# Other orders of steps on four engines in two stages of a fused four-layer transformer kernel

## What is computed

```python
# Layer 1, attention: linear attention with feature map elu(t) + 1
q, k = elu(q) + 1, elu(k) + 1
kv   = einsum('bhnd,bhne->bhde', k, v)
x    = x + (q @ kv / (q . k_sum + 1e-6)) @ w_out.T
# Layer 1, feed-forward: shared gated net on all tokens, one of 8 experts on 256 tokens
sh         = ln(silu(x @ sw1) * (x @ sw2)); shared_out = sh @ sw3 + sb3
x_moe      = x[index_b, index_t]
top1       = argmax(sigmoid(x_moe @ eg_w.T + eg_b) + exp_bias)
weights    = softmax([sigmoid(shared score), expert score of top1])
expert_out = ln(silu(x_moe @ ew1[top1]) * (x_moe @ ew2[top1])) @ ew3[top1] + eb3
final_out  = shared_out.at[index_b, index_t].set(w0 * shared + w1 * expert_out)
# Layer 2, feed-forward (in stage Last): low-rank experts, y = gelu(x A1) B1, A2, B2, weighted by token
# Layer 3, attention part (in Last): x @ W1 + causal depthwise convolution(x, 21 taps) @ W2 + bias
# Layer 3, feed-forward (in Last): 4-bit quantized gated net
xq   = fp4_quant_dequant(x);  h = silu(xq @ wgq.T) * (xq @ wuq.T)
out  = fp4_quant_dequant(h) @ wdq.T
```

## Time and profile before

| what | value |
| --- | --- |
| device time, three runs | 1425.2, 1425.36, 1428.38 us; median 1425.36 us |
| span of the profiled execution | 1426.4 us |
| busy of the span: PE, DVE, ACT, POOL | 1370.7, 1205.4, 1101.6, 283.0 us |
| stage Layer1 in the trace (first step to the last addition to X) | 399 to 550 us |
| stage Attention2 in the trace | 550 to 1178 us |
| stage Last in the trace | 1178 to 1426.4 us |

### The profile page before, as it was taken

The page is one execution under the profiler, slowest core; times in us unless marked ns, Lnnn a source line. Parts: engine busy times, 40 slices in busy tenths (PEclk is TensorE's granted clock), DMA queues, the critical chain, the costliest instruction groups (busy, mean ns, idle before and its releaser), DMA issues.

```text
span 1426.4 us, 25921 instructions
## 1 busy us (share of the span) xinstructions
PE 1370.7 (96%) x9689; PEld 675.9 (47%) x9689; DVE 1205.4 (85%) x2663; ACT 1101.6 (77%) x2071; POOL 283.0 (20%) x239
## 2 busy tenths in 40 slices
PE   5999999999989998999999999999999999999998
PEld 4552332322258885333343333443333345566796
DVE  6898876785389979999999999888888869999997
ACT  4678989899957724888878888888888877887545
POOL 5210010000033321111211011111011113234452
PEclk9999999999999999999999999999999999999999
DMA  4238788767610001000000000000000000000000
GB/s 113 41 92 173 159 193 190 170 134 170 147 57 1 1 1 75 1 1 1 1 1 1 1 1 1 2 1 1 1 2 1 1 30 1 1 9 8 9 16 23
DMA packets 29949, 65.38 MB, mean 46 GB/s; under 512 B 5376, under 2 KB 16896, under 8 KB 28544
## 3 DMA queue, kind: packets, MB, share of 16 engines
q1 hardware_dynamic: 29824, 63.72, 19.0%
HBM read 54.27 MB, written 9.44 MB: 45 GB/s over the span
## 4 chain that ended last, share of the span: by engine, by line
PE 67%; DVE 17%; DMA 5%; POOL 4%; ACT 2%; issue 2%; SPq 1%; DVEq 0%; ACTq 0%; POOLq 0%
PE ps L2028 16%; PE ps L2018 12%; PE ps L516 6%; PE ps L525 6%; PE ps L1997 6%; PE ps L2041 4%; DVE p6ac L2555 3%; PE ps L2008 3%; DMA p1GB<-gscr 2%; PE ps L534 2%; POOL WA L2235 1%; PE ps L2490 1%; POOL WA L2239 1%; DVE st L164 1%; DMA p1R<-tscr 1%
## 5 line engine op out<-in xcount | busy, mean ns | idle before, releaser
L2137 ACT ACTIVATE p4E<-ps,p4mx,p4sc 128x512 f32<-128x512 f32 x512 | 393.4, 778 | 62.6 <-DVE p4mx L2090 60.8
L2085 DVE TENSOR_REDUCE p4mx<-ps 128x2 f32<-128x1024 f32 x205 | 249.7, 1218 | 29.2 <-PE ps L2018 28.1
L2028 PE MATMUL ps<-p4E,p4vn 128*64 128x512 f32 x1024 | 243.0, 599 | 0.2
L2018 PE MATMUL ps<-p4T 64*128 64x512 f16 x1536 | 199.3, 379 | 3.8 <-ACT p4E L2137 3.5
L2160 POOL TENSOR_TENSOR p4vn<-p4v,p4zs 128x512 f32<-128x512 f32 x64 | 66.7, 1042 | 503.4 <-DVE p4zs L2093 469.6
L657 DVE SCALAR_TENSOR_TENSOR p1Pb<-ps,WB,p1GB 128x512 f32<-128x512 f32 x128 | 95.4, 748 | 64.9 <-PE ps L525 55.0
L752 ACT ACTIVATE p1g<-ps,WB 128x1024 f32<-128x1024 f32 x128 | 135.4, 1121 | 12.6 <-PE ps L516 6.6
L516 PE MATMUL ps<-p1R,p1w1s 128*128 128x512 bf16 x512 | 134.0, 381 | 6.4 <-DMA p1R<-tscr 5.3
L2018 PEld LDWEIGHTS ps<-p4T 64*128 64x128 f16 x1536 | 58.3, 94 | 157.1 <-ACT p4E L2137 86.0
L525 PE MATMUL ps<-p1g,WB 128*32 128x512 f32 x512 | 129.1, 601 | 2.9 <-DVE p1Pb L657 2.7
L525 PE MATMUL ps<-xn,WB 128*32 128x512 f32 x256 | 128.3, 602 | 0.2
(11 more groups left out here) (374 smaller groups left out, 2586.0 us busy)
## 6 DMA issues: line engine op xcount, KB each, us to landing
p1GB<-gscr SPq DMA_DIRECT2D x64, 512.0 KB, 7.5
p1R<-tscr SPq DMA_DIRECT2D x64, 128.0 KB, 6.2
gscr<-p1gT SPq DMA_DIRECT2D x16, 256.0 KB, 6.8
tscr<-p1tp SPq DMA_DIRECT2D x24, 128.0 KB
WB<-in_w SPq DMA_DIRECT2D x1, 2560.0 KB, 9.1
X<-in_x SPq DMA_DIRECT2D x8, 256.0 KB, 5.7
out<-X SPq DMA_DIRECT2D x7, 256.0 KB, 2.3
WA<-in_w SPq DMA_DIRECT2D x4, 438.5 KB, 8.6
```

Source lines behind the costliest of these rows:

```text
L2018: y = p.e.matmul(ps[:, banks[hh], :], t[rows, q, 128 * j:128 * j + 128], t[rows, 2 + r, :], start=o == 0, stop=o == 2)
L2028: t = p.e.matmul(ps[64 * hh:64 * hh + 64, self.bank["ctx", n], :], vn[n % 2][:, j, 64 * hh:64 * hh + 64], E[2 * (n % 2) + hh][:, j, :], st ...
L2085: v.e.tensor_reduce(m, ps[:, low:low + 2, :], AX, ALU.max).then_inc(v.own.h, v.one())
L2137: a.e.activation(self.E[2 * i + hh][:, j, :], ps[:, banks[hh], :], ACT.Exp, bias=self.mx[i][:, j, hh:hh + 1], scale=pre.sc[:, 1, 0:1], acc ...
```

## The change

Eight strings change, four in Layer1 (PE, DVE, ACT, POOL) and four in Last. Each new string has the same letters as the old one as often as before, so that each engine issues the same steps; SP's strings, the steps themselves, the waits that each carries and the numbers of filler products are untouched. The items of a step keep their order. What changes besides the order is what hangs on it: the PSUM bank of each PE step, and where ACT's tables change (in Layer1 and at the start of Attention2 the table loads go from 7 to 5, since the router's sigmoid and exponential now stand otherwise among silu and the rest, and the load ahead of L2137 is no longer needed; in Last they go from 12 to 8).

```diff
--- before.py
+++ after.py
@@ -1019,17 +1019,17 @@
     }
     ORDER = {
         "tensor": (
-            "abcccccccddeabfaegbccccccfeghfhccgdddhbaabiejcccccciciiiifiieagfhbiigejhfiijddgbahiibiiaeiiijifjeiigfhiigjkhkk"
-            "iiiiiiiijljlkmnnlommmmmmmnolknkklknlnlklnnlpppnppqqqqrrrqqqrrrq"),
+            "cbcaccccedcccfbcdcaabgccecehfdfdcbagagbedechfahdfbegiicafhigiehdjijrgbiabiifcchiipkigiceijifjikrhgcchiijikkill"
+            "iiiiikiniijijiiiinlmmooklmlnjmkmknmmnmlkllnnlnppnppqqqrqqrqqrqr"),
         "vector": (
-            "sstcsutvwcccctxexcccsuyztwuescccccytzweshytzhAccBhcAAwiuBiBiiieiisccccccucciwtyzeicccicicyzuhiiwecihcyziAciiBi"
-            "wiihAiuiBiwiAeciuByzecyzhiiiiiiiAhACBCDBDEECFDmCEnmmmmmmmmmmmnDonEmmmmoooCnDoCEDCoEnCoDnDoEEoConnDpEnppppxqrxx"
-            "rqxrrxxrqqrqqqq"),
+            "cscscscutcwectscytzcswuvutewciceccchcyztycsziwiiiuiuAteewyshBzuhAiywezBtyuAhizehcBiixiiiwiAcciiAyzciuciBhBiwie"
+            "AiCBDyzEChcDihcAciiiEAcBiCiCicDciiiBDiEcxFECcmmnDmmcoEnooocommComDCmnDEonCDmmEnEomCmcDoomEcpnmnmnnmcppppcqxrqx"
+            "rxqrxrxqxrqqqqr"),
         "scalar": (
-            "aGtbHtIdtdaGbHIaGtgbHItgtgdddBbHaGIaBBGIbHjtccccccccccccccccccccccccccccgIaGcbHgjccjddgbHBIaGbHBIcaGcjBjggjkkB"
-            "Bkjlljkmlommmmmmmmmmmolkkklkllkllppprrrrrr"),
+            "cbcHaGItdctdbHacccGIIabcGcgHcttdtrbdHaGIaIGgbHdcgtaIGccBdbHcgaIGBgtjjcdcbHccgpcaIbGccHBBkcgkcjjgBckBjkclBcBjkc"
+            "jrlmmcmoccmmolkljkcmmlklkmmlmlmcmlcppcrrrr"),
         "gpsimd": (
-            "csssccccccccsssccccccccAJAAJJsccccccccAJAJAJAADJDJDDDDoooooooDDDrrrr"),
+            "csccscccsccosocossAccccJAscAcAcAcAJccccDoDoJcAJDcAcJcDJJDDJDooDDrrrr"),
         "sync": (),
     }
 
@@ -2258,18 +2258,18 @@
     }
     ORDER = {
         "tensor": (
-            "aabcddbecedeefegeceebdgheeeibdcfejgjjjeedeidcejgfeeedkkblkkjmejgcjeeedefgcckkeeeikdkjjjmjebgfeeedekgkkkibmjjjj"
-            "ldifjjkkjjkkbdmdifjjjjkkkkdmdifjjjjkkkkmijjjjkkkkmkkXkkX"),
+            "abacdbceedbfeeedceeecggeeededhibfjjjjeegceeegeedciljjkjjkfeeekddkbmeedfcggeebikkdjjjjceeefdeeeggdiblkjjfkjmkij"
+            "kdjjkjkjmkdikfbkjjjkjdmdifkkkjjjjkmkkikjkjmkjjkkkmkkkkXX"),
         "vector": (
-            "nnoonopppqqqrnrrscstusunuvvwwwwvwwwwwcwtwwwxywwzAwwwcwBCDEwtwwwFzwwwwwwwcxywwAwGwBCzDGEwGwFGHtHwwwwwwwcIwIwJJw"
-            "KGKwzLxyLwAwwBCDEMnGNFwHwtwwGzcwGwwwwHIwIwJJKKxwwLyzcLwcAtwwwwwwwwBCDEGGGHIFJNwGHIwJwKKwzxwLyLwAwwwBCzDEwwwwNF"
-            "wGGHGIGHIJJKKMnLLtxyGGHGwGAwwwwBCDEwHIwFJIJNKKwwLLxwGyGHGGAwwHIwIwBCDEJJwKFNKwLLxyGGHGIAJGHBCDEIJKKFYYNLLGGHGGHI"
-            "IJJKKLZZNLZZ00"),
+            "noponptqownrwswwcwqnwrcwwtpwwqwuwwrwwxywctwwAwwvBwswwCDuzEcszvwwFuwvwwwwwxyGGAwGwwGHBCDHwzIEcwnwwwwwFIJwKzJwKL"
+            "wwLcMwwGtwGnHwGGwIwwxwyHwAJwwItBwwNJwKwCwwLDwwwwEwxFyczwzAtwwwwKwwGGGBGcwCwDEHIJxFwyLwAHBIKCwzDzJwwLEKwwwwFwML"
+            "xGyGnNGAHwwBIwwJGKtCHGIJLGKGwDEHILGFNwJwKLxywGwHGIAwJKwHGBICLDJEKwGwFHINLwwJwKxyGLAGHBCIDJEGKGFHYYNIJLKLGGHINJ"
+            "KGGHILJKZZLZZN00"),
         "scalar": (
-            "aabcOOOtbeceeeetecPeebQtheeeibcejPjjQjeeeticejRReekkebPkkjQejtcjeeeeRRcckkeekeiPkjjjQjebtRReeeekPkkkibQjjjjRRi"
-            "tjjkkjjkkbPQRRijjjjkkkkPQRRijjjjPkkkkQRRijjjjkkkkRRkkkk"),
+            "abtcOabceOtebeeeceePetOcQeeeehibjjjjPeeceQeeeeRRicjjjjkkeektePkbeReQtceekkiPbjjjjtceQeReeePeRiQRbjkjjkkjkPiRjk"
+            "jjkjRtQRkibkjkjjkPjRQRiRjkkkjPjjkQkRikkRjkjkjjRkkkRkkkk"),
         "gpsimd": (
-            "SnnnnSnySTUSyTUSVWyVWnTUSVWyVWTUSVWyVWTUnVVWSWyTUVWVWyTUVWVWyVVWW"),
+            "nSSnnSnySTUyTUnVWVnWyVWSTyUTVyWUSVWTVUynWSVWVTUWVWySVWTUVWyVWVWVW"),
         "sync": (
             "NNNNNNN00"),
     }
```

## The result

The changed kernel takes 1431.32 us (median of 12 runs, 1429.49 to 1434.6) against 1426.02 us of the kernel before in the same series (12 runs, 1424.76 to 1428.38): a ratio of 1.0032, with a 95% interval of 1.0023 to 1.004. It is slower, by 4.6 us by the ratio and 5.3 by the medians. The forecast was 1414.5 us, within 1405 to 1424, and faster. Its profiled execution has a span of 1432.8 us, 6.4 more than the 1426.4 of before; it is the longest of its twelve (1434.6 us), so that the traces show a little more loss than the medians.

The account below looks back on a forecast made before the run. PE was taken as busy 1370.7 of 1426.4 us, PE and DVE as nearly full in Last. Layer1 -5.7, Attention2 -1.3, Last's middle 0 and end -3.8 sum to -10.8: span 1415.6, median 1414.5 us, range 1405 to 1424.

Parts of the forecast that it names:

- Layer1, -5.7: Layer1's head and end together: 5.7 us less, between -8 and 0.
- 1.4 + 3.9: Layer1: 1.4 us from no DVE wait at L864, 3.9 us from DVE work moved behind L1353.
- The rival of eight blocks of waits at the feature maps: Layer1: PE's reserve is used up, 12 waits in eight blocks cost 21 us, giving 1435.5 us; chance 0.08.
- Attention2, -1.3: Start of Attention2: ACT's table load ahead of the first exponential goes, 1.3 us less, between -1.57 and 0.
- the sign: Start of Attention2: if right, L2137 has no table load and the first PE wait is under 0.3 us.
- Last, the middle, 0 within 3: Middle of Last: four table loads gone are hidden, shuffled taps, quantization and products count 0, between -3 and +3 us.
- a rival with a chance of 0.06: Last: POOL holding a port stalls one more L2555 in each of 8 blocks, +9 us, giving 1423.5; chance 0.06.
- Last, the end, -3.8: End of Last, from the last block's LayerNorm on: 3.8 us less, between -5.7 and +1.
- -2.8 - 1.5 - 1.4: End of Last: L176 earlier on POOL, less DVE work ahead of it, and fillers no longer holding turn x.
- The term of -1.4: End of Last: L2509 behind turn x, fillers begin earlier, so turn x comes 1.4 us earlier.
- the +1.9 that was counted: End of Last: +1.4 us for moved L2509 and transposes, +0.5 for the last block but one.
- Two of its own signs of being wrong: Last: L2555's mean away from 844 ns; turn x to the end over 2 us longer than 23.

Follow-up runs that it names:

- before_silu: The kernel before with the gelu of Last's low-rank net replaced by silu, so that 11 of 12 table loads in Last go; ratio 0.9994 to the kernel before.
- the pow runs: before_pow and after_pow: POOL's L2235 and L2239 in Last replaced by narrow powers, in the kernel before and the changed kernel; ratios 0.9952 and 0.9862.
- after_tail: The changed kernel with 15 DVE steps behind the last block's LayerNorm statistics in another order, L189 and quantization of x first; ratio 1.0032 to the kernel before.
- l1_pool: The new Layer1 with the old Last, but POOL's L176 of the last block ahead of L2235 and L2239 of quant h 11; ratio 0.9938 to the kernel before.
- l1_fill: The new Layer1 with the old Last, and 16 fillers ahead of the L2509 group that PE waits 2.03 us for; ratio 0.9946 to the kernel before.
- layer1_only: The four new strings of Layer1 with the old strings of Last; ratio 0.9958 to the kernel before.
- after_fill: The changed kernel with 16, 20 and 36 fillers ahead of PE's three longest waits in the second half of Last; ratio 1.0012 to the kernel before.
- after_pow: The changed kernel with POOL's L2235 and L2239 in Last replaced by powers of 4 to 7 columns; ratio 0.9862 to the kernel before.
- before_pow: The kernel before with POOL's L2235 and L2239 in Last replaced by powers of 4 to 7 columns; ratio 0.9952 to the kernel before.

## Why the prediction failed

**Layer1, -5.7: right.** Measured -5.4 to the first product of Attention2. From the last addition to X of Layer0 on it is 151.7 and 146.6 us, -5.2, and in both of these traces PE runs at half clock once. The nine other traces with the new Layer1 have no half clock in it and take 145.2 us, and the one with the old Layer1 that has none (before_silu) takes 151.3: -6.1. The pieces: no wait at L864; L1353 4.7 us earlier (for 1.4 + 3.9 = 5.3), the end of the differences 5.9 earlier (for 6.3), and 0.5 given back behind it (for 0.6). The rival of eight blocks of waits at the feature maps did not come: from the end of Layer0 to the first L1997 DVE waits 10.5 us, for 13.9 before.

**Attention2, -1.3: right,** -1.0 measured, the load gone. PE's wait there is 1.23 us for 1.57, though, and not under 0.3 as the sign had it. The drain that the Trainium skill adds ("ScalarE: Activation LUTs", What ACT_TABLE_LOAD costs) is not seen: the measured gain is under the load's own 1.28 us.

**Last, the middle, 0 within 3: here it failed.** It measured +10.7. The step that failed was to count 0 for another order of steps, with "POOL's work is the same, so the mean should stay" as the reason, by which DVE's stretch was held to be the same in each order. PE's idle time in Last, from which the range of 3 us was drawn (11 us by the window), nearly doubled: its waits went from 10.0 to 20.2 us. Two things were wrong in the step. The stretch did not stay: 32 us for 24. And above all its price changed: in the old order DVE's stretch lay where it would have waited for PE (7 us for 19 us of it by the pow runs), in the new one nearly each us of it counts (24 for 26). The slower clock is a smaller part, 2.5 us of the 12.7 of Last. I had read PE at 235.81 and DVE at 228.81 of 247 us as "both full", and did not ask what part of DVE's busy time was work: 24 us of it were not, so that the old order was PE's.

The rule was on the table, as a rival with a chance of 0.06 and a worst case of +9 that was set on top of -10.8. The rows since show the mechanism: L2555, L2216, L2230, L189 (two SBUF inputs) and L170, L2208, L2551 (one, in the form TENSOR_SCALAR) are stretched beside L2235, L2239 and L212; instructions with an input in PSUM, reduces, reciprocals and L164 are not; powers of a few columns, nearly as long on POOL, stretch nothing. That the rival's +9, one more L2555 in each block, is near the loss of this stretch is luck in part: L2555 has 5 us more of stretch, L2216 7 more, and L189 and L170 have 8 less (L189 takes 0.233 us on average for 0.618). The Trainium skill ("SBUF — State Buffer", SBUF: two separate sides) says that the shared port pair is held for a whole instruction, by GpSimd or by a DVE instruction in a 2-port perf mode or with two SBUF inputs (the latter only against a GpSimd instruction that reads SBUF), and that the other waits. The stretched rows agree with it. The narrow powers agree in one direction only: they read SBUF too and hold up nothing that is seen, but are themselves held up by DVE. Worked through, POOL's 66 us of Last had to be weighed against which DVE steps stand beside them, in both orders.

**Last, the end, -3.8: failed,** +2.1 measured. L176 starts 0.08 us behind L170, and the fillers no longer hold turn x, as said. But from the addition behind the mix to turn x it is 14.2 us for 15.5, so -1.3 in place of -5.7 (-2.8 - 1.5 - 1.4): the three were added as if each stood alone on one chain, and DVE's own work is what fills that stretch (after_tail, l1_pool). The term of -1.4 was not on the path of the old order: in l1_fill and layer1_only turn x came 1.5 us earlier and the end did not. The 4.08 us of the 24 L2509, halved to 2.0 for full clock, take 2.92 at full clock, and the half clock was that execution's. The clock hides some of this on both sides: where PE runs at full clock in this stretch, it is 12.5 us in the new order (after_fill) and 14.1 in the old one (layer1_only), which is -1.6 and still far from -5.7. From turn x on it is 25.4 for 23.0, +2.4 for the +1.9 that was counted. The mix at half clock adds 1.0, behind a wait for taps of which the prediction knew nothing. Two of its own signs of being wrong came: the mean of L2555 away from 844 ns (894), and turn x to the end over 2 us longer than 23.

## What to carry over

An engine that is busy nearly all of a stage may not be working: compare mean and median of its instructions, and take what lies between as a wait in disguise. When another order is judged, it is not enough that each engine has the same steps; count beside which of its neighbour's instructions they run, and whether the engine that is slowed has slack in that place. In this kernel the better version is the new Layer1 with the old Last (0.9958; with L176 ahead 0.9938, a further gain that the intervals don't show).

## What the runs showed of the hardware

- Powers of 4 to 7 columns on POOL, 1.0 to 1.5 us in the median, left DVE's instructions beside them at their medians (L2216 of 704 columns in after_pow: at most 0.893 us), where subtractions and products of 704 columns of 1.4 to 1.7 us stretch them to 2.375. So POOL's being busy is not enough. Whether it is the width of the access or the kind of operation is not shown, since both were changed.
- The powers were held up in their turn. Of the 114 in Last of before_pow and after_pow, 34 took over 0.1 us more than the shortest of their form (up to 2.06 us), and at the start of 33 of these a DVE instruction with two SBUF inputs, or a TENSOR_SCALAR on SBUF, was already running.
- After the same idle time of 2.03 us, PE ran the same group of 24 products once in 4.08 us and once in 2.92: the clock behind a wait may differ from one execution, or kernel, to the next. Behind the same wait of 2.14 us, 20 products took 2.40 us in three traces and 3.6 to 4.5 in eleven.
- 11 table loads of 1.28 us on ACT, gone from one stage, were worth less than can be measured (0.9994, 0.998 to 1.0008).
